# Attention: the score matmuls of the two readers, interleaved with one wait, or in two groups with a wait each

## The reference

```python
def _L1_attn_ref(x, qkv_w, qkv_b, proj_w, proj_b):
    B, N, C = (2, 256, 128)
    H = 16
    HD = C // H
    b, n, c = x.shape
    qkv = x @ qkv_w.T + qkv_b
    qkv = qkv.reshape(b, n, 3, H, HD)
    qkv = jnp.transpose(qkv, (2, 0, 3, 1, 4))
    q, k, v = (qkv[0], qkv[1], qkv[2])
    scale = 1.0 / np.sqrt(HD).astype(np.float32)
    attn = jnp.einsum('bhqd,bhkd->bhqk', q, k) * scale
    attn = jax.nn.softmax(attn, axis=-1)
    out = jnp.einsum('bhqk,bhkd->bhqd', attn, v)
    out = jnp.transpose(out, (0, 2, 1, 3)).reshape(b, n, c)
    return out @ proj_w.T + proj_b
```

## Time and profile before

| | |
|---|---|
| time, median of 3 runs | 950.31 us (948.59 to 959.15) |
| the profiled execution: its own time | 950.33 us |
| its span in the profile | 948.5 us |
| busy: PE, DVE, ACT | 736.4, 718.9, 510.6 us |
| mean granted TensorE clock | 0.875 of full speed |
| attention's first score matmul, last output projection | 578.3 us, 780.4 us |

### The profile page before, as it was taken

The page is one execution under the profiler, slowest core; times in us unless marked ns, Lnnn a source line. Parts: engine busy times, 40 slices in busy tenths (PEclk is TensorE's granted clock), DMA queues, the critical chain, the costliest instruction groups (busy, mean ns, idle before and its releaser), DMA issues. The chain is left out here.

```text
span 948.5 us, 12473 instructions
## 1 busy us (share of the span) xinstructions
PE 736.4 (78%) x4266; PEld 574.5 (61%) x4266; DVE 718.9 (76%) x1459; ACT 510.6 (54%) x978; POOL 83.8 (9%) x91
## 2 busy tenths in 40 slices
PE   6760576675766698999999965678888677999997
PEld 5540465564655576787777854445444346888886
DVE  2468999999999178898897976777777616777775
ACT  3233768677664365577785842455666544232332
POOL 1321000000000028200000007100000000000000
PEclk9895787987888979899998986798989777999999
DMA  5740221212211242020201104000000000000000
GB/s 160 233 170 13 42 36 32 46 29 38 46 23 23 63 143 68 1 91 1 91 0 49 43 0 134 0 2 1 1 1 2 1 1 0 2 12 1 12 12 12
DMA packets 73858, 38.72 MB, mean 41 GB/s; under 512 B 54722, under 2 KB 64708, under 8 KB 73796
## 3 DMA queue, kind: packets, MB, share of 16 engines
q1 hardware_dynamic: 70436, 35.31, 13.5%
q10 hardware_dynamic: 3360, 2.62, 0.9%
HBM read 28.41 MB, written 9.50 MB: 40 GB/s over the span
## 5 line engine op out<-in xcount | busy, mean ns | idle before, releaser
L380 PE MATMUL yps<-AT,xn 128*128 128x256 f32 x256 | 86.6, 512 | 64.1 <-ACT AT L275 64.1
L784 ACT ACTIVATE hT<-hps,b1s 128x512 f32<-128x512 f32 x128 | 87.9, 691 | 63.4 <-PE hps L695 62.3
L380 PEld LDWEIGHTS yps<-AT,xn 128*128 128x128 f32 x256 | 66.4, 266 | 81.8 <-ACT AT L275 68.1
L950 DVE TENSOR_TENSOR hl<-hT,hh 128x512 fp32r<-128x512 f32 x128 | 93.2, 750 | 29.3 <-ACT hh L790 27.6
L1367 DVE TENSOR_REDUCE mx<-s_ps 128x2 f32<-128x512 f32 x128 | 82.3, 685 | 32.1 <-PE s_ps L1129 32.0
L1302 ACT ACTIVATE pt<-st_ps 128x512 f32<-128x512 f32 x128 | 69.8, 600 | 65.4 <-PE st_ps L1139 64.9
L266 ACT ACTIVATE rest<-rest,par 128x264 f32<-128x264 f32 x128 | 53.7, 502 | 84.3 <-DVE rest L447 84.3
L1565 ACT ACTIVATE act_h<-up 128x512 f32<-128x512 f32 x64 | 38.3, 598 | 89.7 <-PE up L1518 89.7
L259 ACT ACTIVATE tap<-cst_s,par 128x328 f32<-128x328 f32 x128 | 72.4, 657 | 0.1
L1649 DVE TENSOR_TENSOR hid<-act_h,up 128x512 f32<-128x512 f32 x64 | 43.4, 685 | 28.1 <-PE up L1518 17.3
L1529 PEld LDWEIGHTS eo<-wc,hid 128*128 128x128 f32 x512 | 61.7, 192 | 2.3
(11 more groups left out here) (240 smaller groups left out, 1687.7 us busy)
## 6 DMA issues: line engine op xcount, KB each, us to landing
kd<-kst SPq DMA_DIRECT2D x16, 512.0 KB, 2.7
wdB<-wdd SPq DMA_DIRECT2D x32, 256.0 KB, 5.2
dW<-kd SPq DMA_DIRECT2D x16, 256.0 KB, 3.1
Ks<-kd SPq DMA_DIRECT2D x64, 33.0 KB, 2.0
dW<-kd SPq DMA_DIRECT2D x64, 32.0 KB, 2.1
w1r<-in_w ACTq DMA_DIRECT2D x5, 256.0 KB, 2.8
w2r<-in_w ACTq DMA_DIRECT2D x5, 256.0 KB, 3.2
XT<-in_x_T SPq DMA_DIRECT2D x4, 256.0 KB, 4.3
```

The source lines that it names most:

```text
L380: last = nc.tensor.matmul(yps[:, b // 2, (b % 2) * L:(b % 2 + 1) * L], xn[:, (n // R8 * GB + b) * 2 + jc, :], AT[:].rearrange("p (h j) t - ...
L784: nc.scalar.activation(hT[k][:], hps[:, k, :], ACT.Gelu, bias=b1s[:, m:m + 1]).then_inc(h_done, 1)
L950: nc.vector.tensor_tensor(hl[s % 2][:, k, :], hT[k][:], hh[s % 2][:, k, :].bitcast(F32), ALU.subtract).then_inc(hl_done, 1)
```

## The change

`scores` issues the four matmuls of L1129 first, behind the waits for their own reader and operands, and then the four of L1139, behind theirs. Number, shapes, tiles and semaphore counts of the matmuls stay as they are.

```diff
                     if n >= 2:
                         pe.wait_ge(s_used, n)
-                if tb in whole:
-                    if s % 4 == 0:
-                        pe.wait_ge(max_added, 2 * tb + s // 4 + 1)
-                    m = 16 * tb + 2 * s
-                    if m >= 2:
-                        pe.wait_ge(p_ready, m)
-                for t in range(2):
-                    if sb_ in whole:
+                    for t in range(2):
                         for k in range(2):
                             h = 2 * s + k
                             rows = slice(32 * (h % 4), 32 * (h % 4) + 32)
...
                             if t == 1:
                                 last.then_inc(s_ready, 1)
-                    if tb in whole:
+                if tb in whole:
+                    if s % 4 == 0:
+                        pe.wait_ge(max_added, 2 * tb + s // 4 + 1)
+                    m = 16 * tb + 2 * s
+                    if m >= 2:
+                        pe.wait_ge(p_ready, m)
+                    for t in range(2):
                         for k in range(2):
                             h = 2 * later(s) + k
                             rows = slice(32 * (h % 4), 32 * (h % 4) + 32)
```

## The result

The kernel with the change takes 955.13 us (median of 20 runs, 949.83 to 958.80) against 949.84 us for the kernel before (20 runs): ratio 1.0049, 95% interval 1.0032 to 1.0066, that is 3.0 to 6.3 us slower. The profiled execution of the changed kernel is its fastest, 949.83 us with a span of 948.0, so the two profiles can't be subtracted as wholes; they are read step by step.

The account below looks back on a forecast made before the run. No engine is full: the attention stage is a ring where PE, DVE and ACT wait for one another. 21 delays of 0.117 and 9 of 0.22 make 4.5 us, so 950.3 + 4.5 = 954.8 us, range 949 to 962.

Parts of the forecast that it names:

- The removed wait is worth nothing: First four score matmuls on PE: their wait for ScalarE had already been met each time, so removing it wins nothing.
- Where slack hides a delay: Full-clock round: delay hidden behind steps 0, 1, 3, 5, 6; on the path in step 2, 4, 5, 7 terms.
- the idles behind steps 2 and 7: VectorE stands idle about 0.8 us (0.81 and 0.80) for ScalarE's chain there, so delay counts on the path.
- The terms of steps 2, 5 and 7: A later exponential delays ScalarE's `high` and VectorE's `split`: one delay each on the path, 0.117 us at full clock.
- What a call costs then: Score call on PE: the second four's first half runs beside the first four's second half, so exponential scores come 0.11-0.12 us later.
- d: Delay of the exponential's scores and later PE work per call: 0.117 us at full clock, 0.22 at half clock.
- the free ride somehow stays: Lower bound of the delay: the second four still run free beside the first four, delay 0.
- The moved wait: Waits now ahead of each four, also two per four in steps 0 and 4: -0.5 to +0.5 us, taken as 0.
- The sum: Whole kernel: 950.3 + 4.5 = 954.8 us, 0.5% slower; chance of this forecast 0.52.
- the 30 terms of d: Delays on the path over rounds 1 to 7: 21 of 0.117 and 9 of 0.22, 4.5 us.
- 21.7: Sign that the forecast is right: rounds of 21.7 us at full clock.
- the prediction's second rival: Score calls: the fours run fully one after the other, 0.43 and 0.73 us late, total 967 us; chance 0.12.

Follow-up runs that it names:

- the tenth experiment: Kernel before with all four ScalarE projection reads ahead of the exponentials, plus the fours apart and the max_added wait ahead of the first four: 939.1 us, ratio 0.9911.
- the sixth experiment: The change with the max_added wait ahead of the first four in step 0 only, still between the fours in step 4: ratio 1.0032 to the kernel before.

## Why the prediction was right, and where not

- *The removed wait is worth nothing*: right. ScalarE had never been the last reader in rounds 1 to 7, and none of the 31 waits of the first four is for it.
- *Where slack hides a delay*: right where it could be tried. Step 4 has none (2.89 to 3.01 us, and the time follows), step 0 hides most of its own; and the idles behind steps 2 and 7 were on the path, 8 us came out of them. The terms of steps 2, 5 and 7 themselves were never tried by the change, since the second four are not late there.
- *What a call costs then*: this step failed. It let the t = 0 half of the second four start with the t = 1 half of the first, d = 0.12 late, in 30 places. They start 0.01 late. Order within PE's list didn't hold back these matmuls on other rows of the array, though the description of the kernel has each engine work its list strictly in order, and "the free ride somehow stays", the lower bound of d, was the truth. The row that could have told was in the forecast's own group: if matmuls of L1139 start in the same hundredth as those of L1129, the rows work side by side and nothing says that they must keep step.
- *The moved wait*, "each way a few hundredths, taken as 0": this is the term that carries the loss. Two waits between the fours, both met before, delay the second four by 0.12 whenever PE has just stopped. Every kernel that has them in step 4 is slower (ratios 1.0049, 1.0061, 1.0032), every kernel without them ties with the kernel before (1.0000, 1.0002, 1.0008). The forecast's 14 times a few hundredths were 12 times 0.12 to 0.17, and on the path, in step 4 of rounds 1 to 6, about 0.7 us.
- *The sum*: 4.5 us forecast, 4.7 measured (ratio 1.0049 of 950). That they agree is luck: the 30 terms of d measured nothing, and rounds at full clock lasted 21.44 us, not 21.7. The step lengths explain 0.23 a round at full clock, at most 1.6 us over seven rounds, an estimate since only round 2 is at full clock in both profiles. Of the other 3 us a part goes with the clock: in the 33 runs of the kernel before beside the sixth experiment a mean clock lower by 0.001 went with 0.63 us, and that experiment's own runs had 0.8738 against 0.8765, which makes 1.7 of its 3.6 us difference of means. Whether the longer rounds lower the clock or chance did is open, so for two thirds of the 4.7 us no cause is shown.
- *The two pages that the prediction drew on*: the Trainium skill, TensorE: Matmul & The Clock Gate, "Part 3: Packing small matmuls", has matmuls start in strict program order. The starts above (L1138 0.21 us ahead of L1122's second half) say otherwise across row groups, and ScalarE's start 673.14 - 672.52 = 0.62 after the call (0.60 before) confirms that the scores were really there. That the compiled list has the fours in the kernel's order is shown by the tenth experiment's step 6, where the second four wait for ScalarE and all of the first four run ahead of them. The Trainium skill, TensorEngine Tiling (Array Packing), "Theoretical Speedup", gives up to 4x for a dimension of 32 or less; the prediction's second rival took from it that two tiles in sequence halve the rate, and that fell for the same reason. The page's own bound was not tried. Where the rows really are shared, the next work came 0.67 after the start in place of 0.44.

## What to carry to other kernels

Before giving each reader a wait of its own, look in the waits view at which reader ends the common wait; if it is always the same one, as here, there is nothing to win. Count the waits that end up between packed matmuls: here one that had been met was free, two cost about 0.1 us each time PE had just stopped, and a wait that is always met could move ahead of the group. The larger gain lay on the other engine's list: ScalarE stood idle for scores while a read that was ready (of the projections) stood behind the exponential in its list. Moving those reads ahead was worth 8 to 10 us, about twice what the change cost.

## What the runs showed of the hardware

Matmuls on different groups of 32 rows ran out of program order: four on one pair of groups and four on the other took 0.44 us together in either order, with starts 0.01 us apart although two matmuls of the first pair stood between. On the same two groups the second four started 0.32 us behind, and the eight took 0.67 us. One met wait ahead of a matmul rode with its weight load and left the start 0.01 us behind; a second one was an instruction of its own, 0.051 us long, and with it the second four came 0.11 to 0.17 us late (once 0.27) if PE had just been released by another wait, and 0.01 if it had not.
